# Row sums from the addition, squares by ScalarE and an output in quarters, in the tail of the picked attention

## What is computed

```python
normed = _ln(hidden_states, g1, b1)
scores = sigmoid(einsum('bld,d->bl', normed, Wr) + br)
_, idx = top_k(-scores, k)              # the picked tokens, k = 188 of 1250
q, kk, v = ...                          # 12 heads of 64
probs = softmax(einsum('blhd,bmhd->bhlm', q, kk) / sqrt(dh))
ctx = einsum('bhlm,bmhd->blhd', probs, v)
attn_out = ctx @ Wo + bo
mix_out = (normed + scores[..., None] * pooled[:, None, :]) @ Wm + bm
merged = where(attn_mask[..., None], attn_out, mix_out)
h = hidden_states + merged
n2 = _ln(h, g2, b2)                     # mean and variance of each row of h
return h + gelu(n2 @ W1 + bf1) @ W2 + bf2
```

## Time and profile before

| | us |
|---|---|
| median of 3 runs | 3081.2 |
| lowest, highest | 3080.12, 3084.13 |
| the profiled execution, its own time | 3084.09 |
| its span, first to last instruction | 3082.3 |
| TensorE busy | 2661.2 (86%) |
| VectorE busy | 2064.4 (67%) |
| ScalarE busy | 1251.1 (41%) |
| GpSimd busy | 316.4 (10%) |

### The profile page before, as it was taken

One profiled execution on the slowest core, in us unless ns is written; L12 is line 12 of the kernel. 1 busy time (PEld: TensorE's weight loads), 2 busy tenths in 40 slices (PEclk: granted clock), 3 DMA queues, 4 the chain that ended last, 5 costly groups with the idle time before them and its releaser, 6 DMA issues. The chain is left out here.

```text
span 3082.3 us, 35163 instructions
## 1 busy us (share of the span) xinstructions
PE 2661.2 (86%) x12748; PEld 2023.6 (66%) x12749; DVE 2064.4 (67%) x2871; ACT 1251.1 (41%) x1508; POOL 316.4 (10%) x159
## 2 busy tenths in 40 slices
PE   7877995888846992999999998899999979998989
PEld 3556882232324992555899997898888746456668
DVE  6775899999962555695689996812676865113555
ACT  1573227888720001011677874223655731002511
POOL 0000000000005873000000000610000000000013
PEclk9998557999966996999999998999999979999979
DMA  1566544311017553641755642634443531001003
GB/s 67 140 174 164 162 134 157 134 50 34 17 34 207 191 175 116 227 174 69 229 158 135 177 119 75 207 105 135 143 131 115 161 105 60 2 31 52 1 28 88
DMA packets 158352, 360.88 MB, mean 117 GB/s; under 512 B 29104, under 2 KB 79736, under 8 KB 157567
## 3 DMA queue, kind: packets, MB, share of 16 engines
q1 hardware_dynamic: 113276, 269.52, 29.1%
q10 hardware_dynamic: 35968, 73.97, 6.8%
q0 software_dynamic: 8960, 15.41, 1.9%
HBM read 275.87 MB, written 82.93 MB: 116 GB/s over the span
## 5 line engine op out<-in xcount | busy, mean ns | idle before, releaser
L1679 PE MATMUL gat_acc<-far_u,gat_ft 125*65 125x512 f32 x720 | 286.7, 539 | 57.9 <-DVE far_u L1747 57.5
L1679 PEld LDWEIGHTS gat_acc<-far_u,gat_ft 125*65 125x65 f32 x720 | 93.8, 142 | 247.0 <-issue 154.1
L1139 PE MATMUL rg_out<-rg_w,rg_hT 128*125 128x384 f32 x720 | 232.6, 486 | 0.0
L2268 PE MATMUL rg2a_acc<-rg2a_value_part,rg2a_wts_part 125*125 125x512 f32 x600 | 205.0, 342 | 14.8 <-DVE rg2a_wts_part L1988 11.4
L2269 PE MATMUL rg2a_acc<-rg2a_value_part,rg2a_wts_part 125*125 125x512 f32 x600 | 205.7, 343 | 0.0
L2270 PE MATMUL rg2a_acc<-rg2a_value_part,rg2a_wts_part 125*125 125x512 f32 x600 | 204.1, 340 | 0.0
L1139 PEld LDWEIGHTS rg_out<-rg_w,rg_hT 128*125 128x125 f32 x720 | 135.0, 188 | 96.6
L1727 DVE TENSOR_TENSOR far_u<-far_u,gat_lowb 125x1250 f32<-125x1250 f32 x120 | 174.6, 1456 | 0.4 <-PEq L787 0.4
L1747 DVE SCALAR_TENSOR_TENSOR far_u<-far_u,counts_u 125x1250 f32<-125x1250 f32 x120 | 174.6, 1455 | 0.0
L1714 ACT ACTIVATE far_u<-gat_rows,gat_ks 125x1250 f32<-125x1250 f32 x118 | 156.8, 1329 | 42.7 <-PE gat_acc L1679 33.6
L370 PE MATMUL sums<-src_hot,key_hot 125*125 125x512 bf16 (+1 forms) x618 | 140.2, 358 | 28.5 <-DVE key_hot L305 27.6
(11 more groups left out here) (498 smaller groups left out, 6100.3 us busy)
## 6 DMA issues: line engine op xcount, KB each, us to landing
rg2a_values<-values_dram SPq DMA_DIRECT2D x89, 384.0 KB, 3.4
rg1a_counts<-counts_dram SPq DMA_DIRECT2D x26, 820.3 KB
rg_mask<-far_dram SPq DMA_DIRECT2D x60, 312.5 KB, 3.4
moe_raw<-in_L_ffn_w SPq DMA_DIRECT2D x16, 1152.0 KB, 5.6
relw_chunk<-in_L_gnn_W ACTq DMA_DIRECT2D x36, 384.0 KB, 3.2
gat_rows<-rows_dram SPq DMA_DIRECT2D x10, 1250.0 KB, 5.7
sorted_dram<-gat_zeros SPq DMA_DIRECT2D x30, 384.0 KB, 9.8
values_dram<-rg_stage ACTq DMA_DIRECT2D x30, 384.0 KB, 2.3
```

What stands on the lines that cost most here:

```text
L1139: last = pe.matmul(self.out_ps[n % 2][:, a, 0:384], self.hT[:, c, t * TP:(t + 1) * TP], self.w_sb[r % 2][:, c, a * 384:(a + 1) * 384], sta ...
L1679: last = pe.matmul(acc[h % 2][0:WIDTH, b, 0:c1 - c0], ft[:, t, h, :], wts[i % HB][:, c0:c1], start=(t == 0), stop=(t == NT - 1))
L2268: pe.matmul(out, still[0], moving[0], start=first, stop=False)
```

## The change

In the tail of `attend_picked`, TensorE raises `out_made` after each half of each group, so four times, and VectorE converts each quarter (94 x 384) when it is made; TensorE waits for eight of the raises of `out_taken`. The addition of a tile to z becomes an operation that also sums the new row (`tensor_tensor_reduce`; in the profile such an operation is CUSTOM_DVE_ANT_0 with a DVE_READ_ACCUMULATOR2_ANT behind it). VectorE multiplies the sum by -1/D, which gives the negative mean, and ScalarE computes (z - mean) squared with a sum over the row, whose 768 squares go to a scratch buffer. The statistics and the aggregation go. In `feed_forward` the variance is that sum by D plus eps, and `rows` adds the negative mean.

```diff
-                last.then_inc(out_made, 1)
-            pe.wait_ge(out_taken, 4)
+                    last.then_inc(out_made, 1)
+            pe.wait_ge(out_taken, 8)
...
-            for q in range(2):
-                dve.wait_ge(out_made, q + 1)
-                high, low = (x[:, q, :].rearrange("p (a b) -> p a b", a=2) for x in out_parts)
-                dve.tensor_copy(high, score_ps[q][0:QT, 0:2, 0:384]).then_inc(out_taken, 1)
-                dve.wait_ge(out_taken, 2 * q + 1)
-                dve.tensor_tensor(low, score_ps[q][0:QT, 0:2, 0:384], high.bitcast(F32),
+            for k in range(4):
+                q, a = divmod(k, 2)
+                dve.wait_ge(out_made, k + 1)
+                high, low = (x[:, q, a * 384:(a + 1) * 384] for x in out_parts)
+                dve.tensor_copy(high, score_ps[q][0:QT, a, 0:384]).then_inc(out_taken, 1)
+                dve.wait_ge(out_taken, 2 * k + 1)
+                dve.tensor_tensor(low, score_ps[q][0:QT, a, 0:384], high.bitcast(F32),
                                   op=ALU.subtract).then_inc(out_taken, 1)
             for t in range(NT):
                 dve.wait_ge(spread, t + 1)
                 z_t = z[:, t, :].rearrange("p (a b) -> p a b", a=2)
-                dve.tensor_tensor(z_t, z_t, score_ps[t % 2][0:TP, 0:2, 0:384], op=ALU.add).then_inc(added, 1)
-                if t >= 1:
-                    dve.wait_ge(added, t)
-                    row_stats(dve, g, z, t - 1)
-            dve.wait_ge(added, NT)
-            row_stats(dve, g, z, NT - 1).then_inc(stats_done, 1)
-            dve.wait_ge(stats_done, 1)
+                dve.tensor_tensor_reduce(out=z_t, in0=z_t, in1=score_ps[t % 2][0:TP, 0:2, 0:384], scale=1.0, scalar=0.0,
+                                         op0=ALU.add, op1=ALU.add, accum_out=g.row_sums[:, 1, t:t + 1]).then_inc(added, 1)
+                dve.wait_ge(added, t + 1)
+                dve.tensor_scalar(g.row_sums[:, 0, t:t + 1], g.row_sums[:, 1, t:t + 1], -1.0 / D, None,
+                                  op0=ALU.mult).then_inc(mean_done, 1)
...
+            act.wait_ge(ctx_made, len(units))
+            squares = probsT[0][:, :, :].rearrange("p t q -> p (t q)")[:, 0:D]
+            for t in range(NT):
+                act.wait_ge(mean_done, t + 1)
+                if t >= 1:
+                    act.wait_ge(squared, t)
+                act.activation(squares, z[:, t, :], ACT.Square, bias=g.row_sums[:, 0, t:t + 1],
+                               accum_out=g.row_sums[:, 1, t:t + 1]).then_inc(squared, 1)
+            act.wait_ge(squared, NT)
...
-                dve.tensor_scalar(n2[:, t, :], z[:, t, :], mean_var[:, t, 0:1], std_inv[:, t:t + 1],
-                                  op0=ALU.subtract, op1=ALU.mult).then_inc(rows_done, 1)
+                dve.tensor_scalar(n2[:, t, :], z[:, t, :], g.row_sums[:, 0, t:t + 1], std_inv[:, t:t + 1],
+                                  op0=ALU.add, op1=ALU.mult).then_inc(rows_done, 1)
...
-            for t in range(NT):
-                last = dve.bn_aggr(mean_var[:, t, :], g.row_stats[:, t, :, :].rearrange("p a b -> p (a b)"))
-            link(last)
-            link(dve.tensor_scalar(var[:, :], mean_var[:, :, 1], eps, None, op0=ALU.add))
+            link(dve.tensor_scalar(var[:, :], g.row_sums[:, 1, :], 1.0 / D, eps, op0=ALU.mult, op1=ALU.add))
```

More of the change, by code:

```diff
@@ L3090, in attend_picked @@
             s.sem(f"att_{x}") for x in ("ctx_made", "ctx_out", "vc", "out_made", "out_taken", "spread", "added"))
-        stats_done = s.sem("att_stats")
+        mean_done, squared = s.sem("att_mean_done"), s.sem("att_squared")
         block = s.block()
@@ L3301, in feed_forward @@
         bias = s.sb("ff_bias", [128, FC])
-        mean_var = s.sb("ff_mean_var", [TP, NT, 2])
         var, inv, std_inv, square = (s.sb(f"ff_{x}", [TP, NT]) for x in ("var", "inv", "std_inv", "square"))
@@ L3583, in build @@
         g.row_stats = s.sb("row_stats", [TP, NT, 2, 6])
+        g.row_sums = s.sb("row_sums", [TP, 2, NT])
         constants(g)
```

## The result

The changed kernel took 3065.72 us (median of 6 runs, 3062.24 to 3072.66), the kernel before 3081.07 us beside it (6 runs). The ratio is 0.9952, with a 95% interval of 0.9939 to 0.9964. That is faster, but by 15.4 us where the prediction said 9.7 (3081.2 to 3071.5), and just outside its range, which ended at 3067.5.

What follows compares the result with a forecast made beforehand. It took TensorE at half clock to bound the spread, after a 2.0 us idle gap. 0.8 + 10.75 + 0.6 + 0.05 = 12.2 off 3084.09 gave 3071.9 us; 3071.5 taken, range 3067.5 to 3080.5.

Steps and rivals of the forecast that it cites:

- (a): Output converted in quarters: first spread matmul 1.18 us behind the projection, gain 0.8 us, bounds 0.6 to 1.0.
- (b): Spread: with 1.2 us idle TensorE's clock stays at 1.00, 80 matmuls take 14.0 us; gain 10.75 us.
- (c): Tail of the spread, last addition to barrier's release: 2.65 us in place of 3.29, gain 0.6 us (0.1 to 0.7).
- (d): Start of the next stage: ten aggregations go, but Sqrt's table load covers nearly all; gain 0.05 us (0 to 0.1).
- (e): Behind the changed code: clock's later steps may move, worth 1.7 us either way; set to zero, kept for the range.
- the other reading of the medians: If the 2.9 us between profiled execution and median lie elsewhere than in the old spread's clock, new median 3069.
- the step from the profiled execution to the median: Whole kernel: 3071.9 us on the profiled execution, 3069 by the other reading of the medians; 3071.5 taken.
- the 2.9 us: Whole kernel: profiled execution of 3084.09 us against the median of three runs, 3081.2 us.
- the clock that falls all the same: Spread: clock falls despite the shorter gap, only 1.45 us gained, 3082.6 profiled or 3079.8 by median; chance 0.22.
- the doubling: Spread: VectorE's addition with its sum costs twice, 2.1 us per tile, total 3079.9 us; chance 0.04.
- the slower case: Spread: addition with its sum takes 3.1 + 0.2 us a tile, as seen while GpSimd worked; total 3093; chance 0.03.

Runs made afterwards that it cites:

- the shifted one: Kernel before with three matmuls of unused result ahead of the output projection, the 2.03 us gap kept: 3072.33 us, 0.9977.
- the sums alone: Changed kernel with the output converted in halves as before, only the sums and squares kept: 3076.93 us, 1.0000; profiled again, 3075.91 us.
- the fillers: Matmuls of unused result in TensorE's idle times: six in kernel before, 3073.43 us; in the changed kernel with the early Sqrt, 3065.76 us.
- the early Sqrt: Changed kernel with one single-element Sqrt on ScalarE ahead of the squares, so its table loads there: 3063.69 us, one run.

## Why the prediction was wrong

(a) Right. Conversions of 0.55 us, first spread matmul 1.23 us behind the projection (1.2 forecast). One bound was reckoned wrong: with a fixed part of 0.25 us in each instruction the gain would be 0.7 us, not 0.6.

(b) Right in mechanism and size: the clock stays at 1.00, 14.35 us for the spread (14.0 + 0.2), VectorE done with a tile in 1.15 us (1.2). From the end of the projection to the start of the last addition it was 26.98 us and is 15.62 us, so 11.4 us with (a), where I had 11.55. The argument was only half right, and the result is in part luck. I read the 1.74 and 1.88 us gaps of the earlier trace rows as two sides of a length; the same 1.88 us at the same place kept the clock in the changed kernel, 2.03 us kept it in the shifted one, and 1.57 us lost it at the place of the change. By length alone the forecast should not have been as sure as it was.

(c) Right: from the start of the last addition to the barrier's release 2969.52 to 2972.16, 2.64 us (2.65 forecast). Square took 0.94 us, not 0.85.

(d) Right: 0.10 us, forecast 0.05, in its bounds.

(a) to (c) together: from the end of the projection to the barrier's release 30.27 us before (2957.17 to 2987.44) and 18.26 us after (2953.90 to 2972.16), 12.0 us, and with (d) 12.1; the sum said 12.2.

(e) This is the first step that failed. I set the later steps of the clock to zero and treated them as chance. They are not: both profiles of before have 41.0 to 41.2 us in the up projections, all three of the change 39.10 to 39.12. In the first profile of each, the up projections spend 1.7 us at 0.50 before the rise instead of 3.4, and the fall before the last three doesn't come. Half of 1.7 us and half of 3.4 us make 2.5 us; measured are 1.9 to 2.1 us in the whole of them, and they belonged into the sum. The rows of one kernel could not tell that they would fall this way and not the other. But the range didn't have them in full either: my own 3069 for the other reading of the medians, less the 1.7 us of (e), is 3067.3, already below its end at 3067.5.

The second is the step from the profiled execution to the median. I supposed that the runs at 3080.12 and 3081.2 us had kept the clock in the old spread, so that the new kernel would not gain the 2.9 us again, and took 3071.5. Those two executions were not profiled, so their clock is not known; both profiles of before and both of the sums alone show 0.50 there. The executions differ ahead of the changed code: the projection's first bias matmul starts anywhere from 2923.7 to 2941.4 in the fourteen profiles, with code that is the same up to there but for the fillers and the early Sqrt. The gain should have been taken off the median: 3081.2 - 12.2 = 3069, and with the 2.1 us of (e) 3067. The measured median lies 1.2 us below that, which is less than the single executions differ among themselves.

The rivals: the clock that falls all the same didn't come, but it was nearer than its 0.22 tells (0.34 us of idle time). The Trainium skill ("TensorE: Matmul & The Clock Gate", "Why this matters for your kernels") asks only for idle gaps below about 3 us. The traces disagree: the clock fell behind 2.03 us in all four profiles of the old place, and behind 1.57 us in one. The addition with its sum took 0.954 us with one source in PSUM, so neither the doubling nor the slower case came; GpSimd was idle, so what it would do to this addition is not shown.

## What to carry to other kernels

Where a stage behind a short wait of TensorE runs at half clock at full occupancy, look at the wait and not at the stage: 0.8 us less idle time was worth 11 us, and 0.34 us more of it lost nearly all again. Removed work beside a slower engine is worth only its tail (about 0.7 us here) until that engine is fast, and then it is worth more (3.6 us). Compare stages, not totals, when the code ahead varies by more than the change gives; and expect that a stage that ends earlier meets the clock's next steps at another place of its work, for better (2.1 us) or worse (1.84 us).

## What was not expected of the hardware

The clock doesn't go by the length of TensorE's idle time alone: 1.57 us let it fall at the place of the change, 2.03 us in the shifted kernel and 1.88 us before the last up projections of the changed kernel did not. And at one place it does the same in every profiled execution, although the code ahead ends up to 14 us earlier or later: four of four falls with 2.03 us unshifted, three of three profiles of the change alike. That the clock's steps ahead tie the later ones to the work would explain it; no run here tests that, and it stays open. Nor was it tried how far below 1.57 us the edge lies at this place.
